# A selective-scan phase: D*u moved to TensorE's accumulation, and one multiply by B in eight to ScalarE and GpSimd

## The reference, cut to what matters

```python
x_proj, z = jnp.split(x @ W_in + b_in, 2, axis=-1)
u = silu(x_proj)
B, C = jnp.split(u @ W_xproj + b_xproj, 2, axis=-1)
dt = jax.nn.softplus(u @ W_dt + b_dt)
# for each token t, per channel and state:
h = h * jnp.exp(dt_t[..., None] * A) + (dt_t * u_t)[..., None] * B_t[:, None, :]
y_t = jnp.einsum('bds,bs->bd', h, C_t) + D * u_t
# then
y = y * silu(z)
out = y @ W_out + b_out
```

## Time and profile before

| | us |
|---|---|
| median of 3 runs | 3417.8 |
| lowest and highest | 3413.84, 3419.44 |
| the profiled execution | 3419.52 |
| its span | 3417.8 |

### The profile page before, as it was taken

The page is one execution under the profiler, slowest core; times in us unless marked ns, Lnnn a source line. Parts: engine busy times, 40 slices in busy tenths (PEclk is TensorE's granted clock), DMA queues, the critical chain, the costliest instruction groups (busy, mean ns, idle before and its releaser), DMA issues. The chain is left out here.

```text
span 3417.8 us, 49267 instructions
## 1 busy us (share of the span) xinstructions
PE 2904.9 (85%) x18868; PEld 1304.3 (38%) x18868; DVE 2744.8 (80%) x3098; ACT 1958.8 (57%) x3506; POOL 1854.0 (54%) x957
## 2 busy tenths in 40 slices
PE   5878879788788788787897848999999999999997
PEld 2222222222222222222221226666666666666664
DVE  2999999999999999999999966666666666666664
ACT  4766676667666666766765435444444444444444
POOL 3798988988989889889889621111111111111100
PEclk8999999999999999999997659999999999999999
DMA  4111111111111111111213140000000000000000
GB/s 144 50 44 59 47 52 48 45 61 42 36 59 47 53 59 47 47 53 39 66 32 113 40 153 8 26 26 25 25 25 25 26 26 25 25 25 25 25 7 13
DMA packets 92545, 153.64 MB, mean 45 GB/s; under 512 B 12001, under 2 KB 29025, under 8 KB 91874
## 3 DMA queue, kind: packets, MB, share of 16 engines
q1 hardware_dynamic: 92386, 151.54, 14.0%
HBM read 92.79 MB, written 58.72 MB: 44 GB/s over the span
## 5 line engine op out<-in xcount | busy, mean ns | idle before, releaser
L713 POOL TENSOR_TENSOR h<-h,c_rep 128x1024 f32<-128x1024 f32 x512 | 1198.8, 2355 | 241.9 <-ACT carry L527 241.7
L643 DVE TENSOR_TENSOR_SCAN h<-r_ps,carry,h 128x512 f32<-128x512 f32 x768 | 943.9, 1275 | 23.4 <-ACT r_ps L521 23.2
L521 ACT ACTIVATE r_ps<-r_ps,decay 128x512 f32<-128x512 f32 x1024 | 631.6, 656 | 321.6 <-PE r_ps L295 321.2
L630 DVE TENSOR_TENSOR h<-u_ps,b_rep 128x1024 f32<-128x1024 f32 x512 | 620.2, 1211 | 25.5 <-PE u_ps L306 24.9
L1522 POOL TENSOR_TENSOR x<-x,rows 128x1024 f32<-128x1024 f32 x32 | 76.4, 2388 | 971.6 <-PE tr L959 971.6
L306 PE MATMUL u_ps<-dtu,spread 32*128 32x512 f16 x2048 | 332.1, 404 | 110.3 <-DVE h L630 109.6
L295 PE MATMUL r_ps<-dt,spread 32*128 32x512 f16 x2048 | 331.7, 403 | 79.6 <-DVE h L643 67.9
L318 PE MATMUL y_ps<-h,gather 128*32 128x512 f32 x2048 | 297.9, 651 | 88.4 <-POOL h L713 87.3
L643 DVE TENSOR_TENSOR_SCAN h<-r_ps,zero,h 128x512 f32<-128x512 f32 x256 | 314.3, 1272 | 12.6 <-ACT r_ps L521 12.5
L40 PE MATMUL nat<-region,act 128*128 128x512 f16 x512 | 204.7, 400 | 94.5 <-DVE act L1376 48.4
L40 PE MATMUL fps<-x,region 128*128 128x256 f16 x1024 | 280.9, 274 | 3.1 <-issue 2.4
(11 more groups left out here) (220 smaller groups left out, 5597.5 us busy)
## 6 DMA issues: line engine op xcount, KB each, us to landing
u_t_dram<-u SPq DMA_DIRECT2D x16, 1024.0 KB, 4.9
z_t_dram<-zs SPq DMA_DIRECT2D x32, 512.0 KB, 2.9
uz<-u_t_dram SPq DMA_DIRECT2D x64, 256.0 KB, 3.8
uz<-z_t_dram SPq DMA_DIRECT2D x64, 256.0 KB, 4.3
y_t_dram<-y SPq DMA_DIRECT2D x64, 256.0 KB, 2.3
y_t<-y_t_dram SPq DMA_DIRECT2D x15, 1024.0 KB, 7.4
x_in<-dram_x SPq DMA_DIRECT2D x16, 512.0 KB, 8.0
result<-x SPq DMA_DIRECT2D x16, 512.0 KB, 3.4
```

The costliest lines, as they stand in the source:

```text
L521: nc.scalar.activation(bank, bank, ACT.Exp, scale=decay[:, col:col + 1]).then_inc(s_da, 1)
L630: nc.vector.tensor_tensor(h[:, g % H_GROUPS, o:o + 2, :], u_ps[:, :, :], b_rep[:, c % 2:c % 2 + 1, :].broadcast_to([P, 2, TS]), ALU.mult). ...
L643: nc.vector.tensor_tensor_scan(row, r_ps[:, 2 * (pair % 2) + o, :], row, start, ALU.mult, ALU.add)\
L713: nc.gpsimd.tensor_tensor(rows, rows, c_rep[:, c % 2:c % 2 + 1, :].broadcast_to([P, 2, TS]), ALU.mult)\
```

## The change

`skip` on ACT multiplies the `u` half of `uz` by D in place; after the second group of a tile PE adds it to `y_ps` by a product with the fp32 identity. The gate on DVE now multiplies `y_ps` by silu(z) and writes the finished y; `finish_y` on POOL goes. Of each eight pairs, the one that is 5 modulo 8 (`ON_POOL`) has no dbu on DVE: ACT copies `u_ps` into `h` (`copy_dtu`, in ACT's step pair-3, behind exps(pair-1)), and POOL multiplies by B in place (`dbu`, in POOL's step pair-3, behind weigh(pair-3)). `rep_dtu` of the pair behind it waits for ACT's copy, and its scans wait for POOL.

```diff
+ON_POOL = 5
+def multiplied(pair):
+    return pair - (pair + 7 - ON_POOL) // 8
+def copied(pair):
+    return (pair + 7 - ON_POOL) // 8
...
 # PE
             def rep_dtu(pair):
                 c, j, p = place(pair)
-                if pair >= 1:
-                    pe.wait_ge(s_m1, pair)
+                if pair % 8 == ON_POOL + 1:
+                    pe.wait_ge(s_ucopy, copied(pair))
+                elif pair >= 1:
+                    pe.wait_ge(s_m1, multiplied(pair))
...
                 if q == 0 and g > 0:
-                    pe.wait_ge(s_gate, g // 4)
+                    pe.wait_ge(s_y, g // 4)
...
                 last.then_inc(s_sum, 1)
+                if q == 1:
+                    n = g // 4
+                    pe.wait_ge(s_skip, n + 1)
+                    if n == 0:
+                        pe.wait_ge(a["s_ident"], 2)
+                    nc.tensor.matmul(y_ps[:, :], a["ident"][:, :], uz[:, n % 2, 0, :], start=False, stop=False)
...
 # ACT
+            def skip(n):
+                act.wait_ge(s_uz[n % 2], 32 * (n // 2 + 1))
+                nc.scalar.activation(uz[:, n % 2, 0, :], uz[:, n % 2, 0, :], ACT.Copy,
+                                     scale=d_skip[:, n % NJ:n % NJ + 1]).then_inc(s_skip, 1)
+
+            def copy_dtu(pair):
+                g = pair // 2
+                act.wait_ge(s_du, pair + 1)
+                if g >= H_GROUPS:
+                    act.wait_ge(s_sum, g - H_GROUPS + 1)
+                o = 2 * (pair % 2)
+                nc.scalar.activation(h[:, g % H_GROUPS, o:o + 2, :], u_ps[:, :, :], ACT.Copy).then_inc(s_ucopy, 1)
...
                 if pair + 2 < TOTAL:
                     exps(pair + 2)
+                if (pair + 3) % 8 == ON_POOL and pair + 3 < TOTAL:
+                    copy_dtu(pair + 3)
+                if pair % 8 == 3:
+                    skip(pair // 8)
...
 # DVE
             def scans(pair):
                 c, j, p = place(pair)
-                dve.wait_ge(s_m1, pair + 1)
+                if pair % 8 == ON_POOL:
+                    dve.wait_ge(s_m1p, copied(pair + 1))
+                else:
+                    dve.wait_ge(s_m1, multiplied(pair + 1))
...
             def gate(n):
-                j = n % NJ
                 dve.wait_ge(s_sum, 4 * n + 4)
-                dve.wait_ge(s_uz[n % 2], 32 * (n // 2 + 1))
                 if n >= 2:
                     dve.wait_ge(s_yout[n % 2], 16 * (n // 2))
-                nc.vector.scalar_tensor_tensor(y[:, n % 2, :], uz[:, n % 2, 0, :], d_skip[:, j:j + 1], y_ps[:, :],
-                                               ALU.mult, ALU.add).then_inc(s_gate, 1)
+                nc.vector.tensor_tensor(y[:, n % 2, :], y_ps[:, :], uz[:, n % 2, 1, :], ALU.mult).then_inc(s_y, 1)
...
-                if pair + 1 < TOTAL:
+                if pair + 1 < TOTAL and (pair + 1) % 8 != ON_POOL:
                     dbu(pair + 1)
...
 # POOL
+            def dbu(pair):
+                c, j, p = place(pair)
+                o = 2 * (pair % 2)
+                rows = h[:, pair // 2 % H_GROUPS, o:o + 2, :]
+                pool.wait_ge(s_ucopy, copied(pair + 1))
+                nc.gpsimd.tensor_tensor(rows, rows, b_rep[:, c % 2:c % 2 + 1, :].broadcast_to([P, 2, TS]), ALU.mult)\
+                    .then_inc(s_m1p, 1)
...
-            def finish_y(n):
-                pool.wait_ge(s_gate, n + 1)
-                nc.gpsimd.tensor_tensor(y[:, n % 2, :], y[:, n % 2, :], uz[:, n % 2, 1, :], ALU.mult).then_inc(s_y, 1)
...
                 weigh(pair)
+                if (pair + 3) % 8 == ON_POOL and pair + 3 < TOTAL:
+                    dbu(pair + 3)
                 for plan, s in producing(pair):
                     produce(plan, s)
-                if pair % 8 == 3 and pair >= 11:
-                    finish_y(pair // 8 - 1)
...
-            finish_y(NC * NJ - 1)
```

More of the change, by code:

```diff
@@ L156, in selective_scan_phase @@
         s_da, s_m1, s_scan, s_carry = sem("a_da_ready"), sem("a_dbu_ready"), sem("a_scanned"), sem("a_carry_saved")
-        s_hc, s_sum, s_gate, s_y = sem("a_hc_ready"), sem("a_summed"), sem("a_skip_added"), sem("a_y_ready")
+        s_ucopy, s_m1p = sem("a_dtu_copied"), sem("a_dbu_ready_pool")
+        s_hc, s_sum, s_y, s_skip = sem("a_hc_ready"), sem("a_summed"), sem("a_y_ready"), sem("a_skip_ready")
         s_uz = [sem("a_uz_loaded_even"), sem("a_uz_loaded_odd")]
@@ L415, in _ @@
             sums(TOTAL // 2 - 1)
-            pe.wait_ge(a["s_ident"], 2)
         @block.scalar
@@ L477, in evacuate_b @@
                 if n >= 2:
-                    act.wait_ge(s_m1, (n - 1) * PAIRS)
+                    act.wait_ge(s_m1, multiplied((n - 1) * PAIRS))
                 nc.scalar.activation(b_rep[:, n % 2, :], src, ACT.Copy).then_inc(s_ev, 1)
```

## The result

The changed kernel takes 3461.2 us (median of 4 runs) against 3418.5 before: ratio 1.0127, interval [1.0114, 1.0140]. Its profiled span is 3459.2 us, 41.4 over before. The forecast was 3417, practically no change, within 3388 to 3445; the kernel is slower by 1.3% and lies 16 us above that range.

The account below looks back on a forecast made before the run. VectorE was taken to bound the whole, GpSimd the 37-pair stretches with dt work. There +27, +2 and +2, elsewhere -26.6 and -5, and -1.3 at the end sum to about -2 us: 3417 us, range 3388 to 3445.

Parts of the forecast that it names:

- GpSimd in D: D, 37 pairs from pair 56 to the next chunk's pair 29: GpSimd also prepares dt and leads; +4.5 us each.
- The last D: Last 37-pair stretch with dt work, without x_low, so GpSimd has 4.2 us less to do: taken as +2 us.
- the term of R: R, the chunk's 27 pairs without dt work: VectorE leads and saves moved multiplies and some stall; -3.8 us each, seven times.
- the last R: Last, longer stretch of pairs without dt work, with four multiplies off VectorE: -5 us.
- the late L630: VectorE's multiply by B, 0.8 us late in the 27-pair stretch, shrinks by some 0.5 as GpSimd's lag enters lower.
- the margin: Handover chain to ScalarE's copy takes 3.5 us; with GpSimd's lag over 1.2 it costs nothing: booked 0, bound 58 us.
- First D: Starting stretch of the scan phase with dt work, 29 pairs, no backlog at entry: +2 us.
- TensorE's product at 0: 64 identity products on TensorE, at most 1.07 us each, 0 to 68 us in all: taken as 0.
- The gate and the end: VectorE's gate stays at 0.64 us, 0.55 from below; finish_y gone after the last gate gives -1.3 us.
- B: Rival, chance 0.22: with ScalarE late, GpSimd idles for the copy at handovers in 37-pair dt stretches; +32 us, 3449.
- C: Rival, chance 0.09: each identity product on TensorE delays the spread, 8 per chunk x 0.4; +26 us, 3443.
- A: Rival, chance 0.27: VectorE's gain stands in 37-pair dt stretches too, as GpSimd's forced holes fill; -1.6 each, 3374 us.

Follow-up runs that it names:

- e1: Changed kernel with no multiply moved, so only the new gate and D*u on ScalarE and TensorE: 3419.7 us, ratio 0.9995 to the kernel before.
- e2: Changed kernel with the old gate, finish_y and D*u, so only the 64 multiplies moved: 3487.4 us, ratio 1.0190 to the kernel before.
- e10: Changed kernel with GpSimd relieved: low halves of dt and dt*u made on 8 of 512 columns, unused: 3384.6 us, ratio 0.9892 to the kernel before.
- e7: Changed kernel with its new gate, but only pairs 37, 45 and 53 of each chunk moved: 3397.7 us, ratio 0.9931 to the kernel before.
- e8: Kernel before, old gate, with only the multiplies of pairs 61, 5, 13, 21 and 29 of each chunk moved: 3511.1 us, ratio 1.0257.
- e6: Kernel before, old gate, with only the multiplies of pairs 37, 45 and 53 of each chunk moved: 3426.5 us, ratio 1.0011.
- e13: Changed kernel with silu of u and its table loads cut to a copy of 8 columns: 3439.4 us, ratio 1.0051 to the kernel before.
- e3: Changed kernel without TensorE's identity product, scaling and wait kept: 3463.3 us, ratio 1.0117 to the kernel before.
- e9: Kernel before with GpSimd relieved: low halves of dt and dt*u made on 8 of 512 columns, unused: 3365.4 us, ratio 0.9850.

## Why the prediction was wrong

*GpSimd in D (+4.5 each):* right, in its working too. Measured +4.5 in four of six and +5.1 and +5.7 in the others; from weigh 56 to weigh 93 GpSimd takes 146.3 us (forecast 146.1), and the lag at the end of D is 6.9 (forecast 7.0). The holes of 2.8 at steps 62 and 72 are still there, the one at 82 is filled but for 0.5, and three of the five scans wait 1.8 to 2.7 us for the new multiply. GpSimd is busy 95% between those weighs, a little under the 96% named as a sign. D of the changed kernel, GpSimd and then VectorE in order of time:

```profile
1060.63 2.35 POOL L755 TENSOR_TENSOR h<-h,c_rep 128x1024 f32<-128x1024 f32 x1 [2.83 <-ACT carry L544]
```

```profile
1107.80 2.46 DVE L680 TENSOR_TENSOR_SCAN h<-r_ps,zero,h 128x512 f32<-128x512 f32 x2 [2.74 <-POOL h L745]
```

e1 and e2 bear the sum out: D follows GpSimd's work, down to VectorE's own 132.0 in e1 and up to 145.1 in e2. In e10 it stops at 131.2, short of VectorE's own 126.4. The last D (+1.8 for +2) was a guess that came true.

*The step that failed is the term of R, -3.8 each:* "VectorE leads. It saves 3 x 1.11 = 3.3", 0.5 more for a late L630, and nothing for what ScalarE and TensorE get added ("So I book nothing", "I take 0"). R cost +0.8 on average instead, and the last R +1.7 instead of -5, together 39 us of the 43 that the terms were low. Its three parts, by the runs, for the seven R together (us):

| part of the term | forecast | measured |
|---|---|---|
| three multiplies less on VectorE | -23 | -13.9 (e1, e7), -15.1 (e8, e2), +5.7 (before, e6) |
| the late L630, by the lag out of D | -3.5 | +11.6 (e7, changed), +14.1 (before, e8), -6.7 (e6, e2) |
| scaling and product | 0 | +7.6 (before, e1), +6.3 (e2, changed), -12.0 (e6, e7) |

The parts do not add up independently of their order; by before, e1, e7, changed they are +7.6, -13.9 and +11.6, which gives the +5.3 measured. So the multiplies did save, but less than their duration, and two things booked at nothing or as a gain cost more than that.

What stands behind it is the margin, which was computed for one handover with every queue empty (3.5 us for a copy due at lag + 2.31, result due at 7.5). In the kernel the copy (1.02) and the scaling (0.72) stand in ScalarE's queue with evacuations and the silu of u, and what waits behind is not only the next exponential: TensorE waits for the evacuations, with the spreads behind it. TensorE's idle time before L40 on x grew from 35.2 to 67.1 us; e1 without the handover has 31.1, e7 with 24 of the 64 has 47.8, e2 with all has 71.8. By e13, somewhat under half of R's miss goes with ScalarE's queue. For the rest there is the start of R, where TensorE has been idle for 4.4 us and the 3.4 us behind that have a granted clock of 0.50; in e7's two kinds of R the multiply behind the product waits 2.06 us with such an interval there and 0.70 without it. How the miss divides exactly stays open, since no run held TensorE's clock fixed.

*First D, +7.9 for +2:* it is not the sum of two parts. D*u alone (e1) has +5.2, the moved multiplies alone +7.1 (e2) or +8.9 (e8), and without the product it is +8.7 (e3). The cause is open.

*TensorE's product at 0:* its bound of 68 us was too low (83.0 measured): in e7 a product takes 1.13 us at a granted clock of 1.00 and 2.02 at 0.50, and the bound had 1.07 for all. That leaving it out brings nothing (e3) agrees with the 0 in the total, but there TensorE's mean clock in R was lower too (0.90 for 0.93 in chunk 3), so this is no proof of the reason given.

*The gate and the end:* the gate takes 0.58 from start to start (1067.05 to 1067.63), between the 0.55 and 0.64 given. The last scan ends 8.1 us before attention's first instruction instead of 9.4, the -1.3 forecast. The other 2.9 of the table's -4.2 were not forecast: the first scan starts 2.2 earlier, and the phase behind the scan is 0.6 shorter, which is within what it varies by from run to run.

*Rivals.* B comes nearest in number (3449), but not in place: it laid the loss on handovers in D, where GpSimd would idle for the copy. GpSimd idled 0.2 us for it in the D shown, and D is the 140.1 forecast without B. A late ScalarE, B's reason, is seen in R, which B left out. C, that the product delays the spread, is seen at the start of R, but the 26 us that it asked for did not come back without the product (e3), at the lower clock said above. A did not appear: D did not get shorter.

## What to carry to other kernels

Look for where the receiving engine leads, by stretch and not by average, and move work only out of the stretches where it does not: the same change restricted to those pairs (e7) turned +1.3% into -0.7%. Even there do not book the full duration of what was moved: of 26.6 us the moves in R brought some 22 in two surroundings and none in a third. The chain of handovers has to be set against everything that stands in those queues, evacuations and what waits behind them included, and not against empty ones; ScalarE was busy only 74% in R, and waits for its exponentials still grew. And measure a part of a change in more than one surrounding: e6 alone would have said that moving a multiply never pays.

## What the runs showed that was not expected

Where TensorE's half-speed intervals fall is worth microseconds: identical instructions of e7 take R in 97.8 or 101.7 us, with 3.4 or 13.7 us of it at half speed. Half-speed time by itself does not set the time of R, though: e3 has 23 us of it on average and takes 102.3, the changed kernel 12 and 101.5. The kernel before lost more than 7 us per chunk, 1.5% of the time, to GpSimd's low halves (e9), on a page that shows GpSimd busy 54% of the span. And the parts of this change do not add up: each is worth something else beside the others.
